# Weight and smoothing loads moved from SyncE's to ScalarE's queue, and one low part a slot sooner on GpSimd

## What is computed

```python
def _ln(x, w, b):
    mu = jnp.mean(x, axis=-1, keepdims=True)
    var = jnp.mean(jnp.square(x - mu), axis=-1, keepdims=True)
    return (x - mu) * jax.lax.rsqrt(var + EPS) * w + b
...
def _gqa(q, k, v):
    scale = 1.0 / np.sqrt(q.shape[-1])
    scores = jnp.einsum('bsghd,btgd->bghst', q, k) * scale
    p = jax.nn.softmax(scores, axis=-1)
    return jnp.einsum('bghst,btgd->bsghd', p, v)
...
ln_out = _ln(hidden_states, ln_w, ln_b)
q = _ln(_fp8_linear_pertensor(ln_out, wq, ...), qln_w, qln_b)
k = _ln(_fp8_linear_pertensor(ln_out, wk, ...), kln_w, kln_b)
v = _fp8_linear_pertensor(ln_out, wv, ...)
core = _gqa(q, k, v)
qx = _ln(_fp8_linear_pertensor(ln_out, wqx, ...), qxln_w, qxln_b)
kx, vx = jnp.split(jnp.einsum('bsi,oi->bso', cond, w_kv_x), 2, axis=-1)
xout = _gqa(qx, _ln(kx, kxln_w, kxln_b), vx)
cat = jnp.concatenate([core, xout], axis=-1)
catq = _div_clamp_fp8(cat, proj_smooth)
return jnp.einsum('bsi,oi->bso', catq, wproj) * (proj_in_scale * proj_w_scale)
...
x = x + xattn(_layernorm(x), ctx)
x = x + ffn(_layernorm(x))     # _qlinear(silu(gate) * up), hidden width 1408
```

## Time and profile before

| | |
|---|---|
| median of 3 runs | 1833.42 us (1830.92 to 1835.13) |
| profiled execution | 1835.97 us, its span 1834.1 us |
| mean granted TensorE clock | 0.973 |
| busy over the span | TensorE 90%, VectorE 74%, ScalarE 77%, GpSimd 59% |
| DMA queue of SP (all plain and transposing transfers) | 237.66 MB, 64.1% of 16 engines |
| slots of the 8 groups | about 120 to 1470 us |

### The profile page before, as it was taken

The page is one execution under the profiler, slowest core; times in us unless marked ns, Lnnn a source line. Parts: engine busy times, 40 slices in busy tenths (PEclk is TensorE's granted clock), DMA queues, the critical chain, the costliest instruction groups (busy, mean ns, idle before and its releaser), DMA issues. The chain is left out here.

```text
span 1834.1 us, 43340 instructions
## 1 busy us (share of the span) xinstructions
PE 1655.5 (90%) x15491; PEld 1237.8 (67%) x15776; DVE 1364.6 (74%) x3172; ACT 1403.9 (77%) x2936; POOL 1086.3 (59%) x1022
## 2 busy tenths in 40 slices
PE   1459999999999999999999999999998479999999
PEld 1337788778778877887887788778776334444444
DVE  8988988997898899889879988998777432323232
ACT  6669999999999999999999999999999343031211
POOL 1147777777777777777777777777777203030202
PEclk9769999999999999999999999999999789999999
DMA  5028768978787787888778778877889980021100
GB/s 167 24 69 139 139 129 161 145 137 141 142 150 133 142 155 148 134 149 158 125 145 154 136 131 160 153 133 131 172 161 178 279 297 1 25 114 69 68 23 23
DMA packets 641005, 240.32 MB, mean 131 GB/s; under 512 B 612640, under 2 KB 612640, under 8 KB 640800
## 3 DMA queue, kind: packets, MB, share of 16 engines
q1 hardware_dynamic: 640800, 237.66, 64.1%
HBM read 65.58 MB, written 20.99 MB: 47 GB/s over the span
## 5 line engine op out<-in xcount | busy, mean ns | idle before, releaser
L971 POOL TENSOR_TENSOR local<-local 128x512 bf16<-128x512 f32 x512 | 607.2, 1186 | 339.4 <-ACT local L880 339.4
L578 PE MATMUL ps_pj<-wide 128*128 128x256 bf16 (+1 forms) x5544 | 585.2, 255 | 12.7 <-ACT local L803 10.8
L578 PEld LDWEIGHTS ps_pj<-wide 128*128 128x128 bf16 x5544 | 470.7, 98 | 125.5 <-issue 12.0
L877 ACT ACTIVATE local<-ps_s,neg_max 128x512 f32<-128x512 f32 x512 | 389.6, 761 | 46.9 <-DVE neg_max L1178 45.9
L626 PE MATMUL ps_o<-v_hi,local 128*128 128x129 bf16 x2048 | 379.9, 223 | 31.2 <-DMA local<-local 29.3
L880 ACT ACTIVATE local<-ps_s,neg_max 128x512 bf16<-128x512 f32 x512 | 392.3, 766 | 13.9 <-DMA local<-local 13.9
L1178 DVE TENSOR_REDUCE neg_max<-ps_s 128x1 f32<-128x512 f32 x512 | 345.8, 676 | 53.6 <-PE ps_s L642 51.5
L628 PE MATMUL ps_o<-v_hi,local 128*128 128x129 bf16 x2048 | 379.4, 220 | 0.0
L627 PE MATMUL ps_o<-local 128*128 128x128 bf16 x2048 | 379.1, 219 | 0.0
L803 ACT ACTIVATE local<-ps_pj,head_rstd 128x128 f32<-128x128 f32 x756 | 238.2, 434 | 44.0 <-issue 40.2
L947 POOL TENSOR_TENSOR head_rstd<-sq_sum,minus_half 128x3 f32<-128x3 f32 x256 | 218.5, 854 | 25.0 <-DVE sq_sum L1114 25.0
(11 more groups left out here) (112 smaller groups left out, 2591.6 us busy)
## 6 DMA issues: line engine op xcount, KB each, us to landing
w_raw<-w_group SPq DMA_DIRECT2D x32, 512.0 KB, 4.3
quantised_heads<-local SPq DMA_DIRECT2D x32, 512.0 KB, 3.2
wide<-quantised_heads SPq DMA_DIRECT2D x4, 4096.0 KB, 13.1
local<-local SPq DMA_TRANSPOSE x640, 3.2
wide<-x SPq DMA_DIRECT2D x8, 1024.0 KB, 11.8
local<-ctx_t SPq DMA_DIRECT2D x4, 1024.0 KB, 5.3
w_raw<-w_proj SPq DMA_DIRECT2D x8, 512.0 KB, 4.5
wide<-w_proj SPq DMA_DIRECT2D x4, 1024.0 KB, 6.1
```

The source lines that it names most:

```text
L578: last = mm(dst[:, at:at + n], lhs, w_at(par, part, c, cross * 512 + at, n), start=(k == 0), stop=(k == len(terms) - 1))
L877: a(p_exp[:, u % 2], ps_s[u % 2][:], ACT.Exp, bias=neg_max[:, u % 4:u % 4 + 1])
L971: tt_(pp[:, u % PP_BUFS, 1], p_exp[:, u % 2], pp[:, u % PP_BUFS, 0], ALU.subtract)\
```

## The change

Two things change. The loads of the next group's weights (slots 0, 10, 20, 30) and of its smoothing factors (slot 22) leave SP's program and stand in ScalarE's, behind the exponentials of the slot. Their waits are the same. And the low part of the turn j = 1 is written on GpSimd two slots after the turn in place of three; j = 0 and j = 2 stay at three.

```diff
-        QK_LAG, FULL_LAG, REST_LAG = 0, 1, 3
+        QK_LAG, FULL_LAG, REST_LAG = 0, 1, (3, 2, 3)
...
@@ the program of SP
-                    for c in prep_at(slot, -PREP_FIRST, last):
-                        sp.wait_ge(w_loaded, 16 * (CH * g + CH + c + FREE))
-                        sp.wait_ge(w_ready, CH * g + CH + c - 1 + W_FREE)
-                        src = wg_chunks[bass.ds(g + 1, 1), c].rearrange("o p n -> (o p) n")
-                        sp.dma_start(raw(c), src).then_inc(w_loaded, 16)
-                    if slot == SMOOTH_SLOT and not last:
-                        sp.wait_ge(y_done, SLOTS * g + UNIT_FREE)
-                        rows = smooth_dram[bass.ds(g + 1, 1)].rearrange("o n -> (o n)").partition_broadcast(P)
-                        sp.dma_start(rsmooth[:, bass.ds(((g + 1) % 2) * (HEADS * D), HEADS * D)], rows).then_inc(smooth_in, 16)
...
@@ the program of ScalarE
+            def load_next(g, c):
+                act.wait_ge(w_loaded, 16 * (CH * g + CH + c + FREE))
+                act.wait_ge(w_ready, CH * g + CH + c - 1 + W_FREE)
+                act.dma_start(raw(c), wg_chunks[g + 1, c]).then_inc(w_loaded, 16)
+
+            def load_smooth(g):
+                act.wait_ge(y_done, SLOTS * g + UNIT_FREE)
+                act.dma_start(rsmooth[:, ((g + 1) % 2) * (HEADS * D):((g + 1) % 2 + 1) * (HEADS * D)],
+                              smooth_dram[g + 1].partition_broadcast(P)).then_inc(smooth_in, 16)
...
                         a(pp[:, u % PP_BUFS, 0], ps_s[u % 2][:], ACT.Exp, bias=neg_max[:, u % 4:u % 4 + 1])\
                             .then_inc(exp_done, 1)
+                    for c in prep_at(slot, -PREP_FIRST, last):
+                        load_next(g, c)
+                    if slot == SMOOTH_SLOT and not last:
+                        load_smooth(g)
...
@@ the program of GpSimd
-                    for q, j in turn_at(slot, REST_LAG, first, last):
-                        qk_rest(q, j, GROUP_TURNS * g + 3 * (2 + q) + j)
+                    for lag in sorted(set(REST_LAG)):
+                        for q, j in turn_at(slot, lag, first, last):
+                            if lag == REST_LAG[j]:
+                                qk_rest(q, j, GROUP_TURNS * g + 3 * (2 + q) + j)
```

## The result

The changed kernel takes 1846.25 us (1845.44 to 1846.79), the kernel before 1832.4 us beside it. The ratio is 1.0078, with an interval of 1.0066 to 1.009: slower by 13.9 us, where 1820.3 was forecast, and 7 us over the top of the range. The profiled execution took 1845.44 us, its span is 1843.6 us, its mean granted clock 0.966.

A forecast was written before the change was run, and what follows sets the result against it. TensorE and ScalarE, both nearly full, were taken to bound the kernel in turns. Gains 9.6 (11.6 - 2.0) + 3.5 - 0 = 13.1 us, from the median 1833.42, gave 1820.3 us; range 1808 to 1839.

The forecast's parts named there:

- Part 1, the gain: TensorE's 26 waits for the low part, 18.0 us, should go; 11.6 us of it counted as gain in eight groups.
- all 0.76 counts: TensorE's wait at 558.47: ScalarE idles 1.20 us behind it, so its whole 0.76 us was counted as gain.
- Part 1, the cost on GpSimd: Lines 971 and 947 come 0.26 to 0.52 us later on GpSimd; past line 803's slack this costs 2.0 us.
- Rival B: GpSimd's low part collides with VectorE's scaling in slots 22 and 30: 13.3 us, time 1833.6, no change; chance 0.17.
- Part 2: SP loses 35 loads, 18.1 us of its queue; fewer late transposes for TensorE gain 3.5 us, ends 0 and 9.2.
- Rival C: Moving the loads brings nothing, as transposes land late by the load's bytes, not SP's queue: 1823.8 us; chance 0.10.
- Part 3: ScalarE's 35 added DMA issues go by under the exponentials: cost 0, ends 0 and 18.1 us.
- rival A: The DMA issues stop ScalarE: 35 cost 18.1 us, time 1838.4 (1848 if they also wait for transposes); chance 0.20.
- the sign that the prediction named: In the five slots ScalarE's next line starts 0.57 us after line 880; a gap of 0.37 or more means rival A.
- the point from which A decides: An issue on ScalarE costing more than 13.1 / 35 = 0.37 us would outweigh the forecast gain.
- an issue also waits out the rest of a transpose: Shared descriptor generator: SP issues transposes 47% of the time, adding 0.28 us per issue on average; time 1848.
- The marks named for rival B: Signs in the profile after: more pieces of line 1032 over 1 us; a group over 164.8 us makes the prediction wrong.

The follow-up runs named there:

- e3: Changed kernel, but in the groups that scale weights the two j = 1 turns whose sooner slot is 22 or 30 stay at lag three; 1828.07 us, ratio 0.9974.
- e6: Changed kernel with VectorE's weight scaling moved to odd slots 7, 11, 19, 23, 27, 31, 39 and 43; 1817.44 us, ratio 0.9915.
- e1: Kernel before with only the low part of j = 1 a slot sooner, all loads still on SP; 1848.82 us, ratio 1.0086.
- e7: Kernel before with VectorE's weight scaling in the odd slots of e6; 1822.83 us, ratio 0.9943.
- e10: e7 with the low part of j = 1 a slot sooner, loads still on SP; 1819.69 us, ratio 0.9928.
- e2: Kernel before with only the loads moved to ScalarE's queue, the low part at lag three for all j; 1830.96 us, ratio 0.9992.
- e5: Changed kernel with VectorE's weight scaling moved to other even slots (10, 12, 18, 20, 28, 32, 40, 42), out of 22 and 30; 1829.15 us, ratio 0.9979.
- e8: Changed kernel with VectorE's scaling pieces cut to 16 of 128 columns, the rest left out; 1843.13 us, ratio 1.0054.
- e9: e8 with the low part at lag three for all j, loads on ScalarE; 1824.24 us, ratio 0.9947.
- e4: Loads on ScalarE and only the two j = 1 turns whose sooner slot is 22 or 30 moved sooner, in seven groups; 1851.16 us, ratio 1.01.

## Why the prediction was wrong, point by point

**Part 1, the gain: right in kind, value wrong.** TensorE's waits went as forecast, but 11.6 us was counted for them and about 3 arrived by the medians. About 2 us of the 11.6 come from scaling by eight the group with the most waits: behind the run's 26 waits the idle time of 1.20 stands seven times, that of 0.37 seven times and that of 0.16 nine times, which by the same rule is 9.4 us. The other step that failed here is "all 0.76 counts": I gave ScalarE's idle 1.20 us for line 1178 to TensorE, since TensorE had waited shortly before. The maximum has two suppliers, the scores and VectorE's own queue, and I didn't look at the second. This is the same place one group later, in the kernel before, behind the 0.77 us of the earlier trace rows: VectorE, then ScalarE.

```profile
722.45 2.27 DVE L1032 TENSOR_SCALAR w_raw<-w_raw,w_mean,wscale 128x128 f32<-128x128 f32 x4
724.64 0.54 DVE L1114 TENSOR_REDUCE sq_sum<-local 128x3 f32<-128x387 f32 x1
...
725.38 0.66 DVE L1178 TENSOR_REDUCE neg_max<-ps_s 128x1 f32<-128x512 f32 x1
```

```profile
726.08 0.69 ACT L877 ACTIVATE local<-ps_s,neg_max 128x512 f32<-128x512 f32 x1 [1.18 <-DVE neg_max L1178]
```

The four pieces take 2.27 us, held by GpSimd, and the maximum starts when VectorE is through with its queue. The kernel before had the collision already, in slot 40. In e3, where TensorE doesn't wait there any more, one piece of this slot is still held: VectorE, then ScalarE.

```profile
721.29 2.03 DVE L1042 TENSOR_SCALAR w_raw<-w_raw,w_mean,wscale 128x128 f32<-128x128 f32 x4
...
723.99 0.66 DVE L1188 TENSOR_REDUCE neg_max<-ps_s 128x1 f32<-128x512 f32 x1
```

```profile
724.68 0.69 ACT L878 ACTIVATE local<-ps_s,neg_max 128x512 f32<-128x512 f32 x1 [0.97 <-DVE neg_max L1188]
```

ScalarE idles 0.97 us instead of 1.18. In the table the slot goes from 2.65 to 2.34, about 0.3 us of the 0.76 counted. In e6, where the scaling has left it, it takes 1.46, though slot 41 behind it then takes 3.26 in place of 2.84; the two together go from 5.49 to 5.18 in e3 and to 4.72 in e6. So more of that idle time was VectorE's scaling than TensorE's wait.

**Part 1, the cost on GpSimd: the wrong reader.** This is the step that failed and turned the gain into a loss. I put 2.0 us on it, for lines 971 and 947 coming late to ScalarE. That didn't show: the wait before line 794 is 27.4 us, before 30.2. What the move cost is VectorE's time in slots 22 and 30, 22.3 us. The idle time of GpSimd was read as free. In slots 22 and 30 it was time in which VectorE's pieces ran at 0.34 us.

**Rival B is what happened, at too low a price.** The place was right, slots 22 and 30. I priced one held piece of 0.95 us extra in each, 13.3 us in all; there are two more held pieces in each, one under line 959 and one under line 978 close behind, which cost 1.53 us in slot 22 and 1.65 in slot 30: 22.3 us. What was held against it, VectorE's 26 idle us in 200, says nothing, since the maximum stands behind the pieces in the same queue, and ScalarE waits for it in that very slot. With its right price and the sizes of the two gains by the medians the sum is 22.3 - 3 - 2 = 17 us on the slow side, where 13.9 were measured. The other slots gave back 8.5 us and not 5; 2.9 of that is the near tie of slot 10, which the profile before lost in three of six groups and the changed kernel's in none. How the rest divides wasn't separated.

**Part 2, the waits went, the gain isn't shown.** 3.5 us was forecast; the medians differ by 1.7 to 2.6. Its mark is in the profiles: TensorE's weight loads wait for a transposed tile for 7.9 us, 11.4 in e1, 8.3 in e7 and 9.4 in e10, all with the loads on SP, and for 1.3 to 4.3 us in the eight kernels with the loads on ScalarE. But the traces show no time gained by it outside slot 10's near tie. Rival C (nothing) can't be excluded, by e2's interval either. One term was read low: SP issues 640 transposes and not 512, 886 us and not 631, which makes its queue fuller than the prediction took it to be.

**Part 3, right, and rival A is out.** The issues cost nothing that can be seen. Line 860 in the timeline above stands 0.01 us behind the start of line 878, and line 881 starts at the usual distance of 0.59 us. In slots 0, 10, 20, 22 and 30 the activation behind line 881 starts as far behind it as in the kernel before, to 0.01 us at the median, which is the sign that the prediction named. The two issuing lines of the changed kernel, in ns:

```profile
L856 ACTq DMA_DIRECT2D w_raw<-w_group x28: 334/334/394, 129.4 to 1203.2; - x28
...
L860 ACTq DMA_DIRECT2D rsmooth<-inverse_smooth x7: 332/333/337, 182.3 to 1181.4; - x7
```

0.334 us where I took 0.517 from SP as a bound; and 0.37 was the point from which A decides, so that even uncovered the 35 issues would be 11.7 us. The estimate by the Trainium skill, "Perfetto Trace Analysis", section "DMA Instruction — HWDGE (DVE, Sync)", that an issue also waits out the rest of a transpose on SP, 0.28 us on average, does not show: 16 of the 35 issues began while a transpose was being issued, one of them with 0.93 us of it to go, which took 0.334 us; the longest of all took 0.394 us.

**The whole.** The forecast added gains of waits by what ended them, put nothing in the sum for GpSimd's influence on VectorE, and left that to a rival. The marks named for rival B, more pieces over 1 us and a group over 164.8 us, are what the profile shows: 55 pieces over 1 us in the seven groups where there were 23, and groups of 166.5 us.

## What to carry to other kernels

Before an instruction is moved into an idle time of GpSimd, look at what VectorE does in that time: if it scales data in SBUF there, each 128x512 subtraction of GpSimd can hold one of its instructions for up to 1.1 us or so, however small that is, and the price is decided by what is queued behind (14 slots with a maximum and sums of squares behind cost 20 us here, and moving VectorE's scaling out of such slots gave 10.4 us alone, in e7, and 15.8 with the change, in e6). A wait is named after its last link: before idle time is booked as a gain, ask whether the engine that ended it was itself waiting or was busy with its own queue, since only in the first case an earlier input helps. And before two single profiles are compared, look for slots that take one of two lengths in the same kernel, as slot 10 does here.

## What the runs showed of the hardware

```profile
L417 SPq DMA_DIRECT2D w_raw<-w_group x4: 328/328/442, 2.0 to 33.8; - x4
```

The end part, from the last exponential on, has the same work in all kernels, and yet two lengths: 376.0 us in the profiled execution of the kernel before (and in e2, e5, e7, e8 within 0.3), 372.3 in the changed one (and 371.7 to 372.5 in e1, e3, e6, e9, e10; 373.8 in e4). The stretches from 40 us after the last exponential on, of the kernel before and then of the changed one, show the difference (columns as in the earlier trace rows):

```profile
1498.08:1508.08 10.00, 2.37 (x10) 1.98 (x11) 6.53 (x16) 3.96 (x4) 1.01 (x1) 0.76 1.00 386
1508.08:1518.08 10.00, 8.12 (x27) 3.58 (x27) 2.14 (x4) 3.16 (x4) 0.00 (x0) 0.56 0.50 191
```

```profile
1511.24:1521.24 10.00, 3.13 (x14) 2.59 (x15) 6.32 (x15) 3.97 (x5) 1.01 (x1) 0.68 1.02 398
1521.24:1531.24 10.00, 8.50 (x41) 4.00 (x40) 2.78 (x4) 4.36 (x6) 1.16 (x1) 0.98 0.48 184
```

TensorE has little to do for 10 us; in the next 10 us the granted clock is 0.56, near the lower of its two levels (1.2 of 2.4 GHz), in the one execution, and 0.98 in the other, with 27 matmuls against 41. This goes with no part of the change, since kernels with and without either part are on both sides. It moves a single execution by 3.7 us, as much as either small part is worth; 0.8 of it has come up before these stretches, the rest within them. The spans of two profiled executions don't settle such a part; the start of the last exponential leaves this out, and by it the collision costs 1471.2 - 1456.5 = 14.7 us at full size and 1465.1 - 1452.0 = 13.1 us with pieces of 16 columns, the sooner low part gains 0.2 us from e2 to e3 and 5.0 from e7 to e10 (what slot 10 and a single group have in these two is told under e10). Why the clock stays low in some executions is open.
